# Two layers of attention: the cross mask in VectorE's maxima, three results on ScalarE, and other distances between the steps

## The reference

```python
q = apply_rope(split_heads(wq @ x + bq))
k = apply_rope(split_heads(wk @ c + bk))
scores = jnp.einsum('bhqc,bhkc->bhqk', q, k) / math.sqrt(K_CHANNELS)
scores = jnp.where(attn_mask == 0, jnp.float32(-10000.0), scores)
p_attn = jax.nn.softmax(scores, axis=-1)
...
mu = jnp.mean(h, axis=-1, keepdims=True)
var = jnp.mean(jnp.square(h - mu), axis=-1, keepdims=True)
(h - mu) * jax.lax.rsqrt(var + LN_EPS)
```

## Time and profile before

| what | us |
|---|---|
| median of 3 runs | 1647.9 (1640.5 to 1651.4) |
| the profiled execution, own time | 1651.0 |
| its span in the trace | 1649.2 |
| attentions of the first layer: first own sum, last norm end | 87.6, 614.0 |
| attentions of the second layer: first own sum, last norm end | 1035.7, 1408.4 |
| PE, DVE, ACT, POOL busy | 1379.6, 979.9, 620.6, 441.0 |

### The profile page before, as it was taken

One profiled execution on the slowest core, in us unless ns is written; L12 is line 12 of the kernel. 1 busy time (PEld: TensorE's weight loads), 2 busy tenths in 40 slices (PEclk: granted clock), 3 DMA queues, 4 the chain that ended last, 5 costly groups with the idle time before them and its releaser, 6 DMA issues. The chain is left out here.

```text
span 1649.2 us, 29414 instructions
## 1 busy us (share of the span) xinstructions
PE 1379.6 (84%) x9381; PEld 906.9 (55%) x9491; DVE 979.9 (59%) x2625; ACT 620.6 (38%) x1413; POOL 441.0 (27%) x612
## 2 busy tenths in 40 slices
PE   2468999999999963899999964688888877699997
PEld 1245666666665531555556633455555643488886
DVE  5367777787776615222222224568878753478886
ACT  0124445545544430223222323346555543334331
POOL 2243342342341101111111013555555420101100
PEclk9689999999999975999999986789999987699999
DMA  3233443443432107521111114755444420300000
GB/s 89 61 67 64 67 73 58 69 74 58 71 69 38 24 12 246 185 77 36 33 33 33 29 40 90 167 115 117 105 109 113 102 57 17 82 1 14 9 5 26
DMA packets 165943, 112.76 MB, mean 68 GB/s; under 512 B 32786, under 2 KB 155922, under 8 KB 165664
## 3 DMA queue, kind: packets, MB, share of 16 engines
q1 hardware_dynamic: 150880, 99.04, 26.9%
q0 software_dynamic: 3408, 9.31, 2.3%
q10 hardware_dynamic: 11504, 2.53, 0.9%
HBM read 46.48 MB, written 12.45 MB: 36 GB/s over the span
## 5 line engine op out<-in xcount | busy, mean ns | idle before, releaser
L893 ACT ACTIVATE first_probs<-pair 128x512 f32<-128x512 f32 x320 | 189.3, 598 | 221.8 <-PE pair L409 212.0
L450 DVE TENSOR_REDUCE first_negmax_x<-bank 128x2 f32<-128x512 f32 x256 | 172.6, 681 | 51.9 <-PE bank L394 50.6
L394 PE MATMUL bank<-kept_stack_cross 96*128 96x256 bf16 x768 | 153.3, 282 | 11.2 <-DVE second_negmax_a L448 2.8
L1920 ACT ACTIVATE second_probs<-pair 128x512 f32<-128x512 f32 x192 | 113.9, 598 | 125.6 <-PE pair L409 103.0
L409 PE MATMUL pair<-kept_stack_cross 98*128 98x256 bf16 x768 | 150.6, 279 | 3.1 <-DMA kept_stack_cross<-second_rows_x 1.1
L1442 PE MATMUL pair<-kept_w,experts_hidden_t 128*128 x312 | 141.1, 595 | 0.0
L450 DVE TENSOR_REDUCE second_negmax_x<-bank 128x2 f32<-128x512 f32 x128 | 88.5, 692 | 57.4 <-PE bank L394 49.6
L394 PEld LDWEIGHTS bank<-kept_stack_cross 96*128 96x128 bf16 x768 | 74.7, 102 | 74.5 <-issue 23.6
L1483 ACT ACTIVATE experts_hidden_t<-bank,kept_b 128x128 f32<-128x128 f32 x156 | 44.4, 367 | 187.4 <-PE bank L1417 187.4
L1397 POOL DMA_INDIRECT experts_expert_rows<-x_mid,kept_row_of x39 | 37.1, 951 | 276.4 <-PE bank L1409 250.1
L1442 PEld LDWEIGHTS pair<-kept_w,experts_hidden_t 128*128 128x128 f32 x312 | 59.9, 192 | 75.6 <-issue 75.6
(11 more groups left out here) (449 smaller groups left out, 3081.7 us busy)
## 6 DMA issues: line engine op xcount, KB each, us to landing
kept_stack_self<-first_parts_a SPq DMA_DIRECT2D x128, 64.0 KB
kept_w<-in_L_ffn_W SPq DMA_DIRECT2D x16, 512.0 KB, 9.1
kept_w<-in_L_ffn_W SPq DMA_DIRECT2D x8, 1024.0 KB, 9.5
kept_stack_self<-second_parts_a SPq DMA_DIRECT2D x128, 64.0 KB
kept_stack_cross<-first_parts_x_k SPq DMA_DIRECT2D x96, 64.0 KB
kept_stack_cross<-first_parts_x_q SPq DMA_DIRECT2D x96, 64.0 KB
kept_stack_cross<-second_parts_x_k SPq DMA_DIRECT2D x96, 64.0 KB
kept_stack_cross<-second_parts_x_q SPq DMA_DIRECT2D x96, 64.0 KB
```

The lines of the kernel that those rows point to most:

```text
L394: mm = pe.matmul(out, q, k, start=mask is None, stop=True, skip_group_check=True)
L450: return dve.tensor_reduce(negmax[:, 2 * n:2 * n + 2], bank[:, :].rearrange("p (m t) -> p m t", t=D), AX.X, ALU.max, negate=True)
L893: act.activation(probs[i % RING][:, :], key_bank[i % 2][:, :], ACT.Exp, scale=att.scale).then_inc(probs_made, 1)
L1920: act.activation(probs[i % RING][:, :], key_bank[i % 2][:, :], ACT.Exp, scale=att.scale).then_inc(probs_made, 1)
```

## The change

In the first layer the cross scores are put into the bank without a mask, and DVE adds the mask as it reduces: for each half of a bank one `tensor_tensor_reduce` writes -(score + mask) to a scratch tile (16 of them, in turn) and keeps the minimum of it, which starts from 3e38. The keys' side keeps its mask matmul. `copy_v`, `own_end` and `cross_end` move to ACT, the latter two as x * rstd - mean * rstd. For that `root` computes -mean and its product with rstd as well, on POOL, with a drain between, and the sums wait for the norm end of the batch before, which still reads the row. In both layers the numbers of the slots are new. In the second the negative maxima of cross attention have two buffers, and the drain at the end of each slot of DVE is gone.

```diff
-OWN_SCORES, CROSS_SCORES, OWN_KEYS, CROSS_KEYS = 0, ((44, 16),), 11, ((67, 4), (75, 12))
+OWN_SCORES, CROSS_SCORES, OWN_KEYS, CROSS_KEYS = 0, ((44, 16),), 11, ((67, 4), (75, 4), (79, 8))
...
-COPY_CROSS_OUT, CROSS_RECIPS, LAY_RECIPS, SPREAD_SUMS, CROSS_HEADS, MAKE_Y, CROSS_SUM, ROOT_X, CROSS_END = 89, 92, 93, 96, 97, 99, 100, 101, 105
+COPY_CROSS_OUT, CROSS_RECIPS, LAY_RECIPS, SPREAD_SUMS, CROSS_HEADS, MAKE_Y, CROSS_SUM, ROOT_X, CROSS_END = 88, 94, 95, 98, 98, 100, 100, 100, 103
...
-                query_scores(pe, CROSS0, score_bank[i % 2], t["stack_cross0"][b % 3], n, ident16[:, :], mask_q).then_inc(scored, 1)
+                query_scores(pe, CROSS0, score_bank[i % 2], t["stack_cross0"][b % 3], n, ident16[:, :], None).then_inc(scored, 1)
...
+            def copy_v(b):
+                if b >= 2:
+                    act.wait_ge(probs_used, key_lane.group("own", b - 2, 0) + 1)
+                act.wait_ge(v_made, b + 1)
+                act.activation(t["v_self0"][b % 2][:, :, 0:DH], work[:, 0:D].rearrange("p (h c) -> p h c", c=DH), ACT.Copy, scale=s4[:, 2:3])\
+                    .then_inc(v_copied, 1)
...
+            def own_end(b):
+                if b >= 4:
+                    act.wait_ge(xq_rot_made, b - 3)
+                act.wait_ge(rstd_a_made, b + 1)
+                act.activation(x1[b % 4][:, :], sum_a[:, :], ACT.Identity, scale=stats_a[:, 9:10], bias=stats_a[:, 11:12]).then_inc(x1_made, 1)
...
-                pool.tensor_tensor(stats[:, 9:10], stats[:, 8:9], t["minus_half"][:, :], ALU.pow).then_inc(rstd, 1)
+                pool.tensor_tensor(stats[:, 9:10], stats[:, 8:9], t["minus_half"][:, :], ALU.pow)
+                pool.tensor_tensor(stats[:, 10:11], stats[:, 6:7], minus_one[:, :], ALU.mult)
+                pool.drain()
+                pool.tensor_tensor(stats[:, 11:12], stats[:, 10:11], stats[:, 9:10], ALU.mult).then_inc(rstd, 1)
...
-                reduce_maxima(dve, CROSS0, negmax_x[:, :], score_bank[i % 2], n).then_inc(reduced, 1)
+                for a in range(2):
+                    ins = dve.tensor_tensor_reduce(masked[(2 * i + a) % 16][:, :], score_bank[i % 2][:, a * D:(a + 1) * D], t["mask_q"][:, a, :], -1.0, 3.0e38,
+                                                   ALU.add, ALU.min, negmax_x[:, 2 * n + a:2 * n + a + 1])
+                ins.then_inc(reduced, 1)
...
+                if b >= 1:
+                    dve.wait_ge(x1_made, b)
                 dve.scalar_tensor_tensor(sum_a[:, :], bank_a[:, 0:D], qo[:, 3:4], x0[b % 3][:, :], ALU.mult, ALU.add).then_inc(sum_a_made, 1)
...
                     latent_end(b)
-                dve.drain()
```

More of the change, by code:

```diff
@@ L549, in first_layer_attentions @@
         negmax_x, two_x = sb("negmax_x", [P, 2 * XG]), sb("two_x", [P, P], BF16)
+        masked = [sb(f"masked_{a}", [P, D], BF16) for a in range(16)]
         rows_a, rows_x = sb("rows_a", [4 * SELF0.groups, P], BF16), sb("rows_x", [4 * CROSS0.groups, P], BF16)
@@ L656, in _ @@
             ident, ident16 = t["ident"], t["ident16"]
-            mask_q, mask_t = (t[n][:, :, :].rearrange("p a k -> p (a k)") for n in ("mask_q", "mask_t"))
+            mask_t = t["mask_t"][:, :, :].rearrange("p a k -> p (a k)")
             def turn_rows(b, s):
@@ L980, in _ @@
                     copy_heads(b)
+                if (b := slots.batch_at(s, OWN_END)) is not None:
+                    own_end(b)
+                if (b := slots.batch_at(s, CROSS_END)) is not None:
+                    cross_end(b)
                 if (b := slots.batch_at(s, COPY_X2)) is not None:
@@ L986, in _ @@
                     scale_qk(b)
+                if (b := slots.batch_at(s, COPY_V)) is not None:
+                    copy_v(b)
                 if (b := slots.batch_at(s, COPY_QK)) is not None:
@@ L1161, in _ @@
                     own_sum(b)
-                if (b := slots.batch_at(s, OWN_END)) is not None:
-                    own_end(b)
-                if (b := slots.batch_at(s, CROSS_END)) is not None:
-                    cross_end(b)
                 if (b := slots.batch_at(s, KEEP_LOGITS)) is not None:
@@ L1171, in _ @@
                     rotate(b, 1)
-                if (b := slots.batch_at(s, COPY_V)) is not None:
-                    copy_v(b)
                 if (b := slots.batch_at(s, ROW_SCALES)) is not None:
@@ L1577, in second_layer_attentions @@
         negmax_a, two_a = sb("negmax_a", [P, 16]), sb("two_a", [P, P], BF16)
-        negmax_x, two_x = sb("negmax_x", [P, 2 * YG]), sb("two_x", [P, P], BF16)
+        negmax_x, two_x = [sb(f"negmax_x_{u}", [P, 2 * YG]) for u in range(2)], sb("two_x", [P, P], BF16)
         rows_a, rows_x = sb("rows_a", [4 * SELF1.groups, P], BF16), sb("rows_x", [4 * CROSS1.groups, P], BF16)
```

70 lines of the change are left out of this document (33 added, 37 removed).

## The result

The changed kernel takes 1580.5 us (median of 4 runs, 1578.8 to 1582.4) against 1649.7 us for the kernel before on the same chip: ratio 0.958 with an interval of 0.953 to 0.963. 1625 was forecast, with a range from 1600. The direction was right, the size was not: 69 us went where 26 had been counted.

The account below looks back on a forecast made before the run. The prediction had PE bounding the first layer, DVE after the change, and neither engine full in the second. From 1651.0 us it took 11 us for the first layer and 14 for the second: 1626, stated as 1625, range 1600 to 1668.

Parts of the forecast that it names:

- What bounds each layer: Both attention rings before the change: PE sets the pace in the first layer, neither engine is full in the second.
- The price c of a masked bank: First layer, DVE: four instructions replacing each reduction cost 0.94 us together, 15.0 us a window.
- The lower bound of 0.78: First layer, DVE: lowest cost expected for a masked bank, 2 x 0.39 us with read-outs free.
- the bound changes sides: First layer after the change: DVE needs 29.9 us a window against PE's 27.2, so DVE sets the pace.
- Rival (a): First layer: read-outs wait for the main instruction to leave the pipe, 1.26 us a bank, about 1694 us; chance 0.13.
- The ends of the first layer: Where the first layer's ring is half full, DVE hides its additions and PE's saving counts: 5 us in all.
- PE's saving of 3.4 us a window: First layer, PE: 16 mask matmuls of 0.215 us each go from every window, 30.6 to 27.2 us.
- Operations moved to ScalarE: First layer: values' copy and both norm ends leave DVE, 1.2 us a window; ScalarE hides their 1.5 us.
- I take a bit over half of one, 0.9 us: 14 us: Second layer: 1.7 us a window from drains and 1.7 from PE's waits, not added; bounds 0 and 26 us.
- The drains: Second layer, DVE: dropping each slot's drain saves 0.17 us at some 10 of 12 slots, 1.7 us a window.
- three wait rows: Second layer, PE: waits of 6.2 + 6.2 + 2.8 = 15.2 us of 190, or 1.7 us a window, removed by new slots.
- Rival (c): First layer: read-outs cost nothing, 0.78 us a bank, window 28.4 us; 1597 us in all; chance 0.10.

Follow-up runs that it names:

- after_pad: Changed kernel with an idle 180-column VectorE addition, about 0.25 us, behind each masked bank of the first layer: 1605.9 us.
- l1_mask_only: Kernel before with the first layer's mask added in the maxima instead of by matmul, old slot numbers, no operations moved: 1647.6 us.
- l1_slots: Kernel before with only the first layer's new slot numbers; mask stays a matmul, no operation moved: 1637.9 us.
- l1_mask_slots: Kernel before with the mask in the maxima and the new slot numbers in the first layer, no operation moved to ScalarE: 1617.2 us.
- l1_mask_recips: Kernel before with the first layer's mask in the maxima and the reciprocals two slots further behind the DMA of the row sums: 1641.7 us.
- l1_mask_recips_k: Kernel before with first-layer mask in the maxima, reciprocals two slots later, and the product of the cross keys also two slots later: 1642.8 us.
- l2_gather: Kernel before with the second layer's indirect gathers moved to come after GpSimd's subtraction, nothing else: 1647.9 us.
- l2_three: Kernel before with only three second-layer distances opened by one slot (turning the rows, product by row, turn of the own output): 1667.0 us.
- l2_nodrain: Kernel before with no drain at the slot's end and two buffers of cross maxima in the second layer, old slot numbers: 1644.1 us.
- l2_three_gather: Kernel before with the three second-layer distances opened and the gathers moved after GpSimd's subtraction: 1641.2 us.
- l2_slots: Kernel before with only the second layer's new slot numbers, keeping the drains and one buffer of maxima: 1620.4 us.
- l1_mask_moves: Kernel before with first-layer mask in the maxima and the values' copy and both norm ends on ScalarE, old slot numbers: 1667.3 us.

## Why the prediction was wrong

**What bounds each layer: right.** In the first PE sets the pace, before and after; in the second neither engine does, and PE's idle time there fell by 24 us.

**The price c of a masked bank: wrong, by itself 25 us.** The step that failed is "c = 2 x (0.39 + 0.08) = 0.94", and with it the bounds: the four instructions cost 0.69 us. I took 0.39 us from start to start as the floor of the main instruction because the nearest row has the same shape, and got 0.345; I took the read-out's 0.08 us as additive, and it lies wholly beside the next instruction. The lower bound of 0.78 was a row of another instruction and not a bound. From it came "the bound changes sides", and that DVE pays back nearly the whole 3.4 us. With 0.69 the same sum has DVE at 25.9 and PE at 27.2 of a steady window of 28.6. Rival (a) falls with the first read-out row, as the Trainium skill's rule for the accumulator read (VectorE: DVE Perf Modes, Two Vector instructions with no wait between them) had it. I had set the same page's other section (The DRAIN you can't avoid) against it, by which the next operation waits for an empty pipe. But that section adds that a next operation that is not held starts earlier, and I left this out. The rows fit the addition: each main instruction starts some 0.07 us before the one ahead of it ends. So the page did not speak for (a), nor for drains that cost nothing.

**The ends of the first layer: counted as 5 us, none seen.** after_pad, at c of about 0.94, has its last cross sum (L1154) only 3 us before that of the kernel before (608.8 against 611.8), where the forecast had -11. It gains 5 us in the ten steady windows, about as I had it. But its first own sum comes 3.6 us later (91.2 against 87.6) and its first three windows take 87.9 us instead of 82.7, which eats up what the last ones gain. From 110 to 150 us the granted clock was 0.66 in after_pad, and 0.66 and 0.74 in the changed kernel, against 0.99 and 0.91 in the kernel before. My sum had no clock in it; that the clock is the reason at the start is likely and not isolated. The larger error of c hid this one.

**PE's saving of 3.4 us a window: right in size, wrong in who can have it.** My sum let it pass whenever DVE had room. With the old numbers it gave 2 us (l1_mask_only), with the new ones 18 (l1_slots to l1_mask_slots). My sum gave the first layer's numbers no term of their own; they are worth 12 us alone, and without them the mask gave 2.

**Operations moved to ScalarE: 1.2 us of DVE a window, priced as part of its bound.** Where DVE doesn't bind they are worth little: 14 against 12 us without the mask, 36 against 30 with it. In the changed kernel ACT was hidden as I said: L974 takes 0.59 us and waited 1.2 us in all for the roots. With the old numbers it was not: the moves cost 19 us beside the mask, and PE waited 11.2 us for L981.

**Second layer, "I take a bit over half of one, 0.9 us: 14 us", bounds 0 to 26: wrong, 38 measured.** The drains gave 8 us. The step that failed is the price of the new numbers, which I took from three wait rows. The three distances I had priced by their wait rows at 15.2 of 190 us lose 16 us when made alone, since turning the rows earlier runs into GpSimd's queue two engines away, which I had not looked at in the second layer. The rest of the table, which I had not priced, holds most of the 30 us. Nor had I priced the clock, whose mean in that stage rose from 0.90 to 0.95 with 18 us less of PE's busy time. The upper bound was the sum of the terms I had named, not what the stage had to give: 28.6 us of PE's idle time in 190, or 3.1 us in each window of 20.9, some 47 us over 15.

**The range.** Rival (c) was the right side at 1597 us, and the range cut half of it off. With the second layer bounded by PE's idle time, (c) would have come to 1651 - 34 - 47 = 1570 us, and 1580 would have been inside, though 0.345 us for a main instruction was below anything that I had written. That the forecast was not further off is partly luck: without the 8 us by which after_pad misses it in the first layer, which erred the other way, it would have been some 1633.

## What to carry to other kernels

In a ring of engines with in-order queues, a wait row tells who came last, not what it would save: the waits removed in l1_mask_recips, l1_mask_recips_k and l2_gather came up under other names for 0 to 4 us, and three distances opened alone cost 16 us until a queue two engines away was cleared. Bound what a new order can give by the idle time of the pacing engine in the stage, not by the rows one can name, and expect that a saving of work may pay only together with the order that lets it through. Add what the clock may give or take back, which none of my terms had. For an instruction that no row shows, take the nearest row as a guess and leave room below it as well as above.

## What the runs showed of the hardware

A masked reduction of 128x256 from PSUM with a mask from SBUF and a bf16 result starts every 0.345 us, less than the 0.39 us of the nearest two-operand instruction with an f32 result, and reading its accumulator out costs 0.08 us that lie fully beside the next one. Two indirect gathers of GpSimd held its queue for 2.3 us. The mean granted clock fell where PE had more gaps. In the second layer, from the first own sum to the last norm end, it was 0.90 (before, l2_three), 0.91 (l2_nodrain), 0.94 (l2_three_gather) and 0.95 (l2_slots, changed kernel). In the first layer, with gaps on PE of 28 and 34 us in 270, it was 0.98 (l1_mask_only) and 0.97 (l1_mask_moves) in that stretch, and with 24 us or less it was 1.00:

```profile
200.00:470.00 270.00, 241.84 (x2230) 152.86 (x2232) 215.36 (x932) 128.54 (x273) 100.03 (x143) 0.98 0.44 68
...
200.00:470.00 270.00, 236.36 (x2167) 149.14 (x2168) 197.25 (x865) 137.74 (x294) 98.74 (x167) 0.97 0.42 65
```
